# Splitting row maxima into three bf16 parts inside 32-bit words, in a two-layer decoder kernel on one core

## What is computed

```python
x = ln(x + L0_attn(x))          # causal self-attention, 16 heads of 8 features
x = ln(x + L0_xattn(x, ctx))    # cross-attention to 154 context rows, 16 heads of 8
x = ln(x + L0_ffn(x))           # 8 experts with a thresholded softmax gate
x = ln(x + L1_attn(x))          # linear attention in chunks of 128, with a causal mask
x = ln(x + L1_xattn(x, ctx))    # cross-attention, 8 heads of 128
x = ln(x + L1_ffn(x))           # gated feed-forward, 384 hidden features
```

## Time and profile before

| | |
|---|---|
| median of 3 runs | 491.49 us (490.01 to 492.0) |
| the profiled execution's own time | 491.0 us |
| its span, first to last instruction | 489.3 us |
| PE busy | 459.8 us, 94% |
| DVE busy | 387.4 us, 79% |
| ACT busy | 345.4 us, 71% |
| POOL busy | 188.3 us, 38% |
| mean granted TensorE clock | 0.985 |

### The profile page before, as it was taken

The page is one execution under the profiler, slowest core; times in us unless marked ns, Lnnn a source line. Parts: engine busy times, 40 slices in busy tenths (PEclk is TensorE's granted clock), DMA queues, the critical chain, the costliest instruction groups (busy, mean ns, idle before and its releaser), DMA issues. The chain is left out here.

```text
span 489.3 us, 11645 instructions
## 1 busy us (share of the span) xinstructions
PE 459.8 (94%) x4048; PEld 305.3 (62%) x4048; DVE 387.4 (79%) x1147; ACT 345.4 (71%) x879; POOL 188.3 (38%) x349
## 2 busy tenths in 40 slices
PE   6687889989999999999999999999999999999995
PEld 5454557655445646666677555667765665896894
DVE  4489988888999899986798888858878678755557
ACT  3535858867768778888648788995866868958742
POOL 8590002650203643444233242434324546835423
PEclk9589999999999999999999999999999999999999
DMA  7841300032210211110002100020000000000001
GB/s 237 196 111 36 95 9 24 13 100 81 57 23 2 67 39 35 39 30 2 3 16 69 32 2 2 4 67 26 2 14 13 0 2 1 1 2 1 1 1 44
DMA packets 27182, 18.35 MB, mean 38 GB/s; under 512 B 8217, under 2 KB 26773, under 8 KB 26997
## 3 DMA queue, kind: packets, MB, share of 16 engines
q1 hardware_dynamic: 23413, 15.44, 11.8%
q10 hardware_dynamic: 3712, 2.17, 1.8%
HBM read 5.58 MB, written 1.05 MB: 14 GB/s over the span
## 5 line engine op out<-in xcount | busy, mean ns | idle before, releaser
L1568 ACT ACTIVATE EX<-psum 128x1024 f32<-128x1024 f32 (+1 forms) x128 | 118.2, 979 | 12.2 <-PE psum L1163 7.4
L1829 DVE TENSOR_REDUCE nmax<-psum 128x2 f32<-128x768 f32 (+1 forms) x96 | 77.3, 862 | 3.8 <-PE psum L1134 3.6
L1824 DVE TENSOR_REDUCE nmax<-psum 128x4 f32<-128x616 f32 (+1 forms) x80 | 67.8, 876 | 3.9 <-PE psum L1127 3.2
L1127 PE MATMUL psum<-K,Q 64*128 64x154 bf16 (+4 forms) x512 | 46.3, 265 | 6.0 <-DMA Q<-xparts 2.0
L1022 POOL TENSOR_TENSOR GP<-REST,xrs 128x512 f32<-128x512 f32 (+1 forms) x48 | 33.2, 715 | 46.6 <-DVE xrs L2066 32.9
L1156 PE MATMUL psum<-Q,K 64*128 64x512 bf16 (+3 forms) x320 | 41.5, 315 | 3.5 <-DMA Q<-mrows 1.1
L1651 ACT ACTIVATE REST<-psum,nxmax 128x154 f32<-128x154 f32 x96 | 36.3, 397 | 10.2 <-DVE nxmax L2056 8.2
L1472 ACT COPY pvraw<-psum 128x512 f32<-128x512 f32 x32 | 18.7, 584 | 33.0 <-PE psum L1190 24.1
L1190 PE MATMUL psum<-EX,V 128*32 128x256 f32 (+3 forms) x512 | 37.7, 435 | 0.0
L1127 PEld LDWEIGHTS psum<-K,Q 64*128 64x128 bf16 x512 | 18.4, 94 | 28.4 <-issue 17.7
L950 POOL TENSOR_SCALAR rstd_rest<-moments_rest 128x2 f32<-128x2 f32 x32 | 7.3, 229 | 74.6 <-DVE moments_rest L1872 74.2
(11 more groups left out here) (345 smaller groups left out, 1165.2 us busy)
## 6 DMA issues: line engine op xcount, KB each, us to landing
Q<-xparts SPq DMA_DIRECT2D x24, 128.0 KB
Q<-parts SPq DMA_DIRECT2D x21, 128.0 KB
K<-parts SPq DMA_DIRECT2D x21, 128.0 KB
X<-in_x SPq DMA_DIRECT2D x4, 256.0 KB, 3.1
Q<-in_L_xattn_Wkv SPq DMA_DIRECT2D x1, 1024.0 KB, 6.6
K<-xkparts SPq DMA_DIRECT2D x24, 38.5 KB
out<-XB_rest SPq DMA_DIRECT2D x6, 128.0 KB, 1.8
Q<-in_L_xattn_Wq SPq DMA_DIRECT2D x1, 512.0 KB, 4.2
```

The source lines that it names most:

```text
L1127: last = mm(to[:, r, at:at + n], Q6[a][p, b % 2, 2 * g + jj, P * q:P * q + P], K6[a][p, b % 2, 2 * g + jj, 0:n], start=at == 0 or bool(a), ...
L1568: drains(nc.scalar.activation(dst, src, ACT.Exp), key)
L1824: last = vec.tensor_reduce(nmax[:, :, :, q], src[:, :, 0:2 * n].rearrange("p r (j k) -> p r j k", j=2), AX.X, ALU.max, negate=True)
L1829: last = vec.tensor_reduce(nmax[:, :, jj, q], src[:, :, at:at + P * (q + 1)], AX.X, ALU.max, negate=True)
```

## The change

The tiles nmax and nrest are gone. mparts becomes fp32, with the same 2 x 80 columns. The reduces write the negated maxima straight into the words of part 0 in mparts. `high(t)` views a tile of 32-bit words as pairs of bf16 and takes the upper one of each pair, that is every second bf16 column: the upper half of an fp32 number is that number cut to bf16. A first subtraction writes word 1 = word 0 less its upper half, a second writes word 2 = word 1 less its upper half, and the two casts are gone. The transpose on PE reads the upper halves only, 80 bf16 columns that lie 4 bytes apart. The wait for the transpose of the turn two before moves from after the last reduce of a turn to ahead of its first. Apart from that the tile causal becomes bf16: POOL writes it so, and the eight multiplications at L2012 read it so.

```diff
+        def high(t):
+            return t.bitcast(BF16).rearrange("p (c w) -> p c w", w=2)[:, :, 1]
...
-        causal = sb("causal", [P, P])
+        causal = sb("causal", [P, P], BF16)
...
-        nmax = sb("nmax", [P, 2, 2, NB])
-        nrest = sb("nrest", [P, 2, 8])
-        mparts = sb("mparts", [P, 2, 80], BF16)
+        mparts = sb("mparts", [P, 2, 80])
...
                 fills_(nc.tensor.transpose(to[0:80, 0:64].bitcast(BF16),
-                                           mparts[:, parity(b, a, g), :], identb[:, :]), key)
+                                           high(mparts[:, parity(b, a, g), :]), identb[:, :]), key)
...
                 src, pieces = pair(key), PIECES[a][u]
+                mine = mparts[:, parity(b, a, g), 0:48]
+                three = mine.rearrange("p (r a m) -> p r a m", r=2, a=3)
+                nmax = mine.rearrange("p (r a j q) -> p r a j q", r=2, a=3, j=2)[:, :, 0, :, :]
+                if u == 0 and before(b, a, g):
+                    b0, a0, g0 = before(b, a, g)
+                    filled(dve, (b0, "mT", a0, g0))
...
                 if u == len(PIECES[a]) - 1:
                     drained(dve, key)
-                    if before(b, a, g):
-                        b0, a0, g0 = before(b, a, g)
-                        filled(dve, (b0, "mT", a0, g0))
-                    m = nmax[:, :, :, :].rearrange("p r j q -> p r (j q)")
-                    three = mparts[:, parity(b, a, g), 0:48].rearrange(
-                        "p (r a m) -> p r a m", r=2, a=3)
-                    step(vec.tensor_copy(three[:, :, 0, :], m))
+                    tops = high(mine).rearrange("p (r a m) -> p r a m", r=2, a=3)
+                    step(vec.tensor_tensor(three[:, :, 1, :], three[:, :, 0, :], tops[:, :, 0, :],
+                                           ALU.subtract))
                     now()
-                    step(vec.tensor_tensor(nrest[:, :, :], m, three[:, :, 0, :], ALU.subtract))
-                    now()
-                    step(vec.tensor_copy(three[:, :, 1, :], nrest[:, :, :]))
-                    now()
-                    vec.tensor_tensor(three[:, :, 2, :], nrest[:, :, :], three[:, :, 1, :],
+                    vec.tensor_tensor(three[:, :, 2, :], three[:, :, 1, :], tops[:, :, 1, :],
                                       ALU.subtract).then_inc(mparts_ready, 1)
```

## The result

The changed kernel took 488.06 us (median of 17 runs, 486.12 to 490.62) against 491.03 us for the kernel before in the same series (17 runs, 489.06 to 494.69). The ratio is 0.9948, with a 95% interval of 0.9934 to 0.9961: 2.6 us faster, between 1.9 and 3.2 us. Two further series with the same kernel gave 0.9949 (0.9925 to 0.9973) and 0.9958 (0.9939 to 0.9976). The forecast was 489.7 us, 1.8 us under a median of 491.5; the range of 487.3 to 492.3 us holds the time.

What follows compares the result with a forecast made beforehand. PE's own work was taken to bound the kernel, idle only 12.0 us between 30 and 400 us. Terms of -1.8 + 0 + 0 + 0 + 0 against a 491.5 us median gave 489.7 us; range 487.3 to 492.3 us.

Steps and rivals of the forecast that it cites:

- What bounds it: Between 30 and 400 us PE's own work bounds the kernel; PE is idle for only 12.0 us.
- Step 1: Two casts gone per split: it ends 0.42 us earlier; seven PE waits for DVE shrink, 1.8 us gained.
- Next in line is then ACT: After shortened waits, ACT or PE's queue limits; nothing deducted, since omitted waits under 0.15 us stand against it.
- second rival: Nothing gained, for cover: PE waits for ACT's exponentials or the maxima rows' DMA instead; 491.5 us, chance 0.11.
- Step 2: The two subtractions read operands at 4-byte steps: zero taken; upper bound 0.43 us lost per split.
- Step 3: Reduces write into mparts, and the transpose wait moves ahead of the first reduce: zero for both.
- Step 4: PE's transposes load bf16 weights 4 bytes apart: zero taken, upper bound 2.4 us lost over 32 loads.
- Step 5: Causal factors in bf16, eight multiplications at L2012: zero taken, at most 1.0 us of DVE time gained.
- DVE's freed time counts for more: Rival: seven waits without a split in front shrink too; 3.95 us gained, 487.5 us, far end 483.6; chance 0.29.
- The gapped weights: Rival: weight loads ahead of L1199's matmul stall PE by 2.4 us; 492.1 us, or 493.9; chance 0.06.
- the unrelieved DVE: Rival: 4-byte reads cost the two subtractions 0.2 us each, a split lasts as before; 491.5 us, chance 0.04.
- The check that I set: PE idle between 30 and 400 us should be near 10.2 us instead of 12.0 in the profile after.

Runs made afterwards that it cites:

- the four old kernels: Kernel before (491.03 us); changed kernel with two casts put back into the chain (490.35); kernel before with bf16 factors alone (490.26) or the moved wait alone (491.03).
- the two profiles with the 0.80 us: Two profiles of kernels with four instructions per split, one with the moved wait alone (491.03 us); PE stands 0.80 us for the split at the eighth transpose.
- six instructions: Changed kernel with four small dependent casts between the two subtractions, so six instructions per split: 497.59 us, ratio 1.0149 against the kernel before.

## Why the prediction was right, point by point

**What bounds it:** right. PE's work is the same, and its idle time is what shrank: in the four old kernels 12.0, 10.4, 11.0 and 11.6 us between 30 and 400 us, in the three profiles of the new one 9.9, 9.9 and 9.7.

**Step 1, sum -1.8 us:** the rate was right (0.21 us an instruction, shown by the timeline; and with as many instructions as before no gain, shown by the casts put back), and the sum is a little small: 2.2 us from transpose to transpose, 2.6 us (1.9 to 3.2) by the runs. But the sum is better than its terms, and that is partly luck. The 0.42 us at 42.99 us came as 0.4. The 0.20 and 0.21 us at the third transpose came to nothing: the second to the third takes 8.48 us before and 8.55 after, as another wait (ACT's exponentials at 42.86 us, 0.30 us) took their place. The 0.23 us at 178.12 us came as 0.40 from turn 16 to 17. The 0.30 us at 190.11 us came as 0.05, and the 0.21 us at 340.73 us as nothing. What failed in the last is the rule that I used: to go back to DVE's last idle time. In the stretch from 332.1 us DVE came to L2061 just as PE had finished what it waited for, so no idle showed; with the split shorter, DVE now stands there for 0.41 us, and the rest of the stretch starts as late as before:

```profile
335.18 0.29 DVE L2061 TENSOR_TENSOR Y_rest<-psum,X 128x128 f32<-128x128 f32 x1 [0.41 <-PE psum L1427]
```

In place of these terms stands the 1.3 us between the seventh and tenth transpose, of which I had counted 0.23 us (the wait at 117.88 us), because one execution's long DMA wait covered the rest.

"Next in line is then ACT ... I take nothing off for it" was right in sum only: small gains in turns 17 to 28 (0.4 us, waits below the view's 0.15 us) stand against 0.8 us by which the two stretches with DMA waits grew. The cover that the second rival named did come in part: 0.30 us for ACT at 42.86 us and, in one of three profiles, 0.71 us for the DMA of the maxima rows.

**Step 2, operands at 4-byte steps:** zero, right: 175 and 176 ns. **Step 3, the moved wait:** zero, right, shown alone. **Step 4, the gapped weights:** zero, right: 113 to 120 ns for each load, so the bound of 2.4 us has nothing in it. The rule of the Trainium skill (page "SBUF — State Buffer", section "Door 1: The DMA port swizzle") and this row agree. **Step 5, the factors in bf16:** zero, right, shown alone; the Trainium skill's row for tensor_tensor with a PSUM operand (page "VectorE: DVE Perf Modes", section "The perf-mode tier table (the rule you actually need)") agrees with 413 and 414 ns.

**The rivals.** "DVE's freed time counts for more" had a point: two waits for reduces behind the eighth transpose, in which I had seen no split's doing, are 0.46 to 0.68 us in the two profiles with the 0.80 us, 0.39 to 0.41 in the second and third profiles of the changed kernel, and 0.63 and 0.71 with two casts behind. The row that was 39.74 is no such case: it went from 0.45 to 0.32 us, but is 0.37 us with six instructions as well. It was not the likeliest course. The time, 488.1 us, lies between it (487.5) and the forecast (489.7), nearer to the rival; the gain in one series, 2.6 us, lies nearer to the forecast's 1.8 than to the rival's 3.95, since the kernel before itself measured 491.0 us there and not 491.5. The 3.97 us of that rival's far end also hold 1.12 us for the maxima rows, which aren't DMAs of parts. "Nothing is gained, for cover" holds nearly so beyond the change: the next instruction less brings 0.3 to 0.5 us in the stretch and nothing that the runs can tell. The gapped weights and the unrelieved DVE are excluded.

**The check that I set:** PE idle near 10.2 us, found 9.9. It told less than I thought. The kernel with two casts in the chain has 10.4 us without the gain; between 30 and 60 us, at a mean granted clock of 0.94, its PE is busy for 26.5 us, against 25.5 us at 1.00 in the changed kernel's second profile, and so the slower clock hides idle time.

## What to carry to other kernels

Where one engine is busy all the time and a second nearly so, ask how far the second is from the elbow, and find out by adding to it: here two instructions of 0.21 us more per turn cost 3.9 us each, two fewer gave 1.0 us each, the third less gave next to nothing. A row of one profile can be that execution's luck, and can hide a wait that other executions have; next to the edited work, look at what a long DMA wait would uncover if it were absent. And going back to the last idle time of an engine isn't enough: an operation that found its input just ready is a point of attachment as well.

## What was not expected

These instructions of 16 elements cost DVE nearly the same: casts from fp32 174 to 175 ns, copies from bf16 to bf16 171, subtractions 175 to 176, 0.21 us from start to start with the semaphore between them. So two casts from fp32 and two copies in bf16 can stand in for one another as fillers. Without a wait the next one starts sooner: with two casts behind, the first cast starts 0.09 us after the last subtraction, for which it doesn't wait.

The slow stretch of TensorE's clock falls in different places: between 30 and 36 us the mean granted clock is 0.72 in the profile of the kernel before and 1.00 in that of the same kernel with the bf16 factors, and the first transposes lie up to 2.7 us apart (33.7 to 36.5 us). The two latest (36.1 and 36.5 us, with one and six instructions) come after a wait of PE of 3.8 us for the parts of K at 26.7 us, and a granted clock of 0.60 and 0.57 between 30 and 36 us. Whether this makes the spread of some 4 to 6 us among runs of one kernel isn't shown. The stretch between the first transpose and the last lay within 0.7 us for each group of kernels and told the groups apart from one profile each, where the times needed a dozen runs or more.

How the 2.6 us divide between an earlier transpose and less work on DVE rests on one profile. With two casts behind the subtractions about half of the gain stays by the five stretches that shrank, and 0.9 us of 2.6 by the runs, with an interval from 2.0 us faster to 0.1 us slower; the two agree, but the interval is too wide to show it by itself. With four casts behind, all of the gain and 5 us more is lost.
